# Heads of two edge loops: a store and a memset out of the barrier, index loads on SyncE, chunk loads ahead of stores, first rows ahead of chunk 3

## What is computed

```
x = layernorm(x + L0(x));  x = layernorm(x + L1(x))

L0: w   = silu(silu(emb(length) @ w0 + b0) @ w1 + b1) @ w2 + b2      # per edge
    msg = products of w, x_up[src] and the unit vector of the edge     # per edge, 2 x 128
    out = segment_sum(msg, dst) @ W_out / 16
L1: h   = relu(concat(x[src], x[dst]) @ W1[type] + b1[type]) @ W2[type] + b2[type]
    msg = h * sigmoid(concat(x[src], x[dst]) @ attn_w[type] + attn_b[type])
    agg = segment_sum(msg, dst);  GRU(agg, x) + x, then layernorm, gamma, beta
```

## Time and profile before

| | us |
|---|---|
| median of 3 runs | 2268.96 (2262.18 to 2270.72) |
| profiled execution, time | 2275.48 |
| profiled execution, span | 2273.8 |
| busy: TensorE / VectorE / ScalarE / GpSimd | 1808.1 / 1479.4 / 1340.5 / 1602.6 |

### The profile page before, as it was taken

One profiled execution on the slowest core, in us unless ns is written; L12 is line 12 of the kernel. 1 busy time (PEld: TensorE's weight loads), 2 busy tenths in 40 slices (PEclk: granted clock), 3 DMA queues, 4 the chain that ended last, 5 costly groups with the idle time before them and its releaser, 6 DMA issues.

```text
span 2273.8 us, 43703 instructions
## 1 busy us (share of the span) xinstructions
PE 1808.1 (80%) x10012; PEld 1435.9 (63%) x10012; DVE 1479.4 (65%) x3700; ACT 1340.5 (59%) x4414; POOL 1602.6 (70%) x1699
## 2 busy tenths in 40 slices
PE   7497999999999999999857776676766667666674
PEld 4275666676666666666636666666666656666563
DVE  4656556556555556556535677777777777778775
ACT  2486778778777777778624544454544445544442
POOL 2567777777777777777544777777777777777771
PEclk6599999999999999999968998788888888888886
DMA  6522223223233232323256854445455454454451
GB/s 204 146 52 56 73 79 82 77 74 87 74 83 79 74 84 75 81 79 82 70 163 167 218 144 115 115 113 121 108 117 119 108 122 113 114 118 113 116 115 34
DMA packets 222343, 236.65 MB, mean 104 GB/s; under 512 B 73015, under 2 KB 163295, under 8 KB 222157
## 3 DMA queue, kind: packets, MB, share of 16 engines
q0 software_dynamic: 53808, 112.80, 21.5%
q10 hardware_dynamic: 90588, 58.98, 10.2%
q1 hardware_dynamic: 77905, 64.42, 9.5%
HBM read 191.66 MB, written 44.35 MB: 104 GB/s over the span
## 4 chain that ended last, share of the span: by engine, by line
POOL 24%; issue 14%; DMA 5%; PE 3%; DVE 2%; ACTq 1%; ACT 1%; POOLq 0%; SPq 0%; DVEq 0%
POOL gp L601 24%; DMA gp<-p_tab_d,idx 2%; DMA win<-q_tab_d 1%; PE ps_v L1760 1%; PE ps_e L1721 1%; ACTq L1517 1%; DVE hid L1867 1%; DMA q_tab_d<-unit_area 0%; ACT hid L1625 0%; DMA unit_area<-x_t_d 0%; ACT unit_area L1655 0%; DMA q_tab_d<-acc 0%; DVE acc L1955 0%; DMA key_row<-key_row_d 0%; DMA zero<-x_t_d 0%
## 5 line engine op out<-in xcount | busy, mean ns | idle before, releaser
L601 POOL DMA_INDIRECT gx<-node_d,idx x832 | 793.9, 954 | 278.9 <-issue 255.7
L601 POOL DMA_INDIRECT gp<-p_tab_d,idx x832 | 791.2, 951 | 277.2 <-issue 248.9
L673 ACT ACTIVATE msg<-ws,y 128x32 f32<-128x32 f32 x2496 | 550.0, 308 | 75.5 <-DVE ws L652 75.1
L894 PEld LDWEIGHTS ps_a<-hot,msg 128*128 128x128 f32 x3328 | 409.3, 198 | 203.2 <-issue 107.3
L1721 PE MATMUL ps_e<-win,hot_x 128*128 128x129 f32 x1680 | 299.8, 351 | 280.3 <-DVE hid L1867 261.3
L894 PE MATMUL ps_a<-hot,msg 128*128 128x128 f32 x3328 | 432.6, 285 | 70.4 <-DVE msg L661 49.0
L1721 PEld LDWEIGHTS ps_e<-win,hot_x 128*128 128x128 f32 x1680 | 274.8, 256 | 303.0 <-DVE hid L1867 274.9
L655 DVE TENSOR_TENSOR vy<-gx,y 128x768 f32<-128x768 f32 x104 | 99.7, 959 | 354.7 <-DMA gx<-node_d,idx 354.5
L1625 ACT ACTIVATE hid<-hid,score 128x128 f32<-128x128 f32 x832 | 277.6, 393 | 10.1
L1867 DVE TENSOR_TENSOR hid<-ps_e,gp 128x387 f32<-128x387 f32 (+1 forms) x312 | 142.0, 508 | 151.8 <-DMA gp<-p_tab_d,idx 142.5
L634 PE MATMUL ps_w<-w,h 128*128 128x256 f32 x832 | 219.6, 409 | 0.0
(11 more groups left out here) (220 smaller groups left out, 2209.1 us busy)
## 6 DMA issues: line engine op xcount, KB each, us to landing
win<-q_tab_d ACTq DMA_DIRECT2D x416, 64.5 KB
key_row<-key_row_d ACTq DMA_DIRECT2D x102, 256.0 KB, 3.7
gx<-node_d,idx POOLq DMA_INDIRECT x832
gp<-p_tab_d,idx POOLq DMA_INDIRECT x832
p_tab_d<-acc SPq DMA_DIRECT2D x23, 516.0 KB, 3.3
q_tab_d<-unit_area SPq DMA_DIRECT2D x36, 258.0 KB, 4.2
q_tab_d<-acc SPq DMA_DIRECT2D x5, 774.0 KB, 4.5
emb<-emb_d SPq DMA_DIRECT2D x102, 32.0 KB
```

Source lines behind the costliest of these rows:

```text
L601: e.indirect_dma_start(out=buf[:, h, t, :], out_offset=None, in_=table, in_offset=bass.IndirectOffsetOnAxis(ap=idx[:, h, t:t + 1], axis=0) ...
L673: last = e.activation(self.cols[1][:, tile, c, :], self.ws[:, tile, :], ACT.Copy, scale=y[:, c:c + 1])
L894: last = e.matmul(ps_a[:, h, b, :], msgs[h].tile(t, b), hot[:, h, t, :], start=t == 0, stop=t == TPS - 1)
```

## The change

- In `prepare`, the zero tile is stored ahead of the sixteen embedding stores, behind the memset of `zero` (semaphore `clear`). SyncE no longer waits there for the embedding stores: it does so in `edges0`, ahead of the first embedding loads, and ScalarE ahead of each `clear_high`.
- VectorE's wait for `row_st` and its memset of 4228 columns leave `prepare`. ScalarE clears 2052 + 1664 of these columns behind its key-row store; the 512 columns from which that store reads are cleared by VectorE in `edges0`, behind the messages of step 0 and the wait for `row_st`.
- In `edges0`, SyncE loads the indices of steps 4 and 5 first, then waits for the embedding stores, loads two embedding tiles, then the index of step 6, then the weights. In the loop the index load comes ahead of the embedding load; the first four steps stand ahead of the loop, with only the index of step 7 in them.
- In `edges1`, SyncE loads the indices of steps 4 to 7: 4 and 5 behind the windows of step 1, 6 ahead of the store of chunk 4, 7 behind it. ScalarE's first four steps load none.
- The node loads of later chunks go ahead of the chunk's store (`store_first`) or of its third piece (`store_table`); the key rows of steps 2 and 3 go ahead of the windows of step 0.
- ScalarE makes the rows of step 0 behind chunk 2, ahead of chunk 3, and waits for `b_ok` only before the node updates. VectorE clears the place of chunks 0 to 2 behind step 0 and that of chunks 3 and 4 inside step 1.

The diff, cut of declarations:

```diff
@@ -60,6 +60,7 @@
 LAG = 3
 LOOPS = STEPS // SLOTS
 N_LATER = 25
+KEY_AT = 2 * TPS * P + PPS
...
@@ -175,6 +176,7 @@
         h1=m.sb("h1", [P, HALF]), h2=m.sb("h2", [P, HALF]),
         ps_h=m.ps("ps_h", [P, HALF]), ps_x=m.ps("ps_x", [P, 512]), ps_w=m.ps("ps_w", [P, 2, TPS, H]),
         h1_mm=m.sem("h1_mm"), h1_ok=m.sem("h1_ok"), h2_mm=m.sem("h2_mm"), h2_ok=m.sem("h2_ok"), w_mm=m.sem("w_mm"),
+        emb_st=m.sem("emb_st"), row_st=m.sem("row_st"),
...
@@ -361,6 +364,8 @@
                 e.dma_start(start_r.bitcast(i32), a["start"].rearrange("o (j q) -> (o j) q", q=PPS))\
                     .then_inc(ld_row, 16)
 
+                e.wait_ge(clear, 1 + 3 + 1)
+                e.dma_start(dram["emb"][STEPS], k["zero"][0:2 * NB, :]).then_inc(stored, 16)
                 for n, span in enumerate(spans):
                     e.wait_ge(exp_ok, n + 1)
                     first, steps = span.start // HALF, (span.stop - span.start) // HALF
@@ -369,9 +374,7 @@
                         e.dma_start(dram["emb"][at_step:at_step + steps].rearrange("s r n -> r s n"),
                                     emb[2 * NB * g:2 * NB * (g + 1), span].rearrange("r (s n) -> r s n", s=steps))\
                             .then_inc(emb_st, 16)
-                e.dma_start(dram["emb"][STEPS], k["zero"][0:2 * NB, :]).then_inc(stored, 16)
                 e.wait_ge(stored, 16 * 3)
-                e.wait_ge(emb_st, 16 * ECH)
                 e.wait_ge(ld_w, 16 * 10)
...
@@ -421,6 +424,9 @@
                 layer0_silu(e, w, mlp, 2, 2)
                 e.wait_ge(row_ok, 1)
                 e.dma_start(dram["key_row"], key_r).then_inc(row_st, 16)
+                e.wait_ge(clear, 1 + 3 + 1)
+                for span in (slice(0, KEY_AT), slice(keys, scratch)):
+                    e.activation(acc[:, span], k["zero"][:, 0:1].to_broadcast([P, span.stop - span.start]), ACT.Copy)
...
@@ -445,7 +451,7 @@
                 e.memset(w["w1"][:], 0.0).then_inc(clear, 1)
                 e.memset(w["w2"][:], 0.0).then_inc(clear, 1)
                 e.memset(w["b2_1"][:], 0.0)
-                e.memset(k["zero"][:], 0.0)
+                e.memset(k["zero"][:], 0.0).then_inc(clear, 1)
...
@@ -539,8 +545,6 @@
                 e.sem_inc(hits_ok, 1)
                 own.then(e.scalar_tensor_tensor(k["key"][:], k["key"][:], 1.0, hit[:], ALU.add, ALU.mult))
                 own.did(e.tensor_scalar(k["key"][:], k["key"][:], 1.0, None, ALU.subtract))
-                e.wait_ge(row_st, 16)
-                e.memset(acc[:, 0:scratch], 0.0)
                 e.wait_ge(count_ok, 1)
                 e.tensor_scalar(k["n_left"][:], ps_n[:], -1.0, float(P * TILES), ALU.mult, ALU.add)
...
@@ -744,13 +748,13 @@
                     e.sem_inc(gate_x, 1)
                     e.dma_start(dram["x1_t"][:, bass.ds(g * UN, UN)], v["x1_t"]).then_inc(xt_st, 16)
 
-                def steps(i, unit, before, last=False):
+                def steps(i, unit, before, last=False, idx_from=0):
                     for u in range(SLOTS):
+                        if not last and u >= idx_from:
+                            e.wait_ge(landed[u], i * (16 * TPS) + 16 * TPS)
+                            load_idx(i * SLOTS + (u + SLOTS), u)
                         if not last:
                             load_emb(i * SLOTS + u, 1 - u % 2)
-                        if not last:
-                            e.wait_ge(landed[u], i * (16 * TPS) + 16 * TPS)
-                            load_idx(i * SLOTS + (u + SLOTS), u)
...
+                def early_idx(u):
+                    e.wait_ge(landed[u], 16 * TPS)
+                    load_idx(SLOTS + u, u)
+
+                for u in range(SLOTS - 2):
+                    early_idx(u)
+                e.wait_ge(mlp["emb_st"], 16 * ECH)
                 for h in range(2):
                     e.dma_start(emb[:, 1 - h, :], dram["emb"][h + 3]).then_inc(emb_in[1 - h], 16)
+                early_idx(SLOTS - 2)
...
@@ -770,7 +782,8 @@
                 load_x(0)
                 for u in range(SLOTS):
                     e.dma_start(k["idx1"][:, u, :], dram["p_idx"][:, u * TPS:(u + 1) * TPS]).then_inc(k["idx_in1"][u], 16)
-                with e.Fori(0, LAG) as i:
+                steps(0, False, False, idx_from=SLOTS - 1)
+                with e.Fori(1, LAG) as i:
                     steps(i, False, False)
...
@@ -812,6 +825,7 @@
                 assert CLEAR * LAG * SLOTS == T * NACC - v["end"]
 
                 def clear_high(j):
+                    e.wait_ge(mlp["emb_st"], 16 * ECH)
                     e.activation(k["acc"][:, bass.ds(j * CLEAR + v["end"], CLEAR)],
                                  k["zero"][:, 0:1].to_broadcast([P, CLEAR]), ACT.Copy)
...
-                e.sem_inc(acc_own, 2)
+                e.sem_inc(acc_own, 1)
...
@@ -1098,8 +1112,11 @@
                 e.tensor_copy(ps_a[:, :, IOTA, :], spread(k["iota"][:, 0:P], 1, 2)).then_inc(iota_ok, 1)
                 e.wait_ge(iota_ok, 1)
                 one_hot(0, 0)
-                for u in range(SLOTS):
-                    messages(0, u, first=u == 0)
+                messages(0, 0, first=True)
+                e.wait_ge(mlp["row_st"], 16)
+                e.memset(k["acc"][:, KEY_AT:KEY_AT + TPS * P // 2], 0.0).then_inc(acc_own, 1)
+                for u in range(1, SLOTS):
+                    messages(0, u)
...
@@ -1535,18 +1553,19 @@
                         load_xq(c + 2)
 
                 def store_first(c):
+                    next_xq(c)
                     e.wait_ge(q_ev, 2 * CH * (c + 1) + 2)
                     if c >= CH:
                         e.wait_ge(q_first[c % CH], 16 * (c // CH))
                     e.dma_start(q_g[:, c * CH:(c + 1) * CH, :], first_buf[:, c * CH:(c + 1) * CH, :])\
                         .then_inc(q_first[c % CH], 16)
-                    next_xq(c)
 
                 def store_table(c):
                     for s in range(CH):
+                        if s == CH - 1:
+                            next_xq(c)
...
 
                 for s in q_st:
                     e.sem_inc(s, 16)
@@ -1554,15 +1573,26 @@
                     load_xq(c)
                 for h in range(2):
                     load_row(e, h, h)
-                for c in range(2):
-                    store_first(c)
-                    e.wait_ge(q_first[c], 16)
-                    load_windows(e, regs, c, c)
+                def early_idx(u):
+                    e.wait_ge(landed[u], 16 * TPS)
+                    load_idx(e, SLOTS + u, u)
+
+                store_first(0)
                 for h in range(2):
                     e.wait_ge(hx_ok, h + 1)
                     load_row(e, h + 2, h)
+                e.wait_ge(q_first[0], 16)
+                load_windows(e, regs, 0, 0)
+                store_first(1)
+                e.wait_ge(q_first[1], 16)
+                load_windows(e, regs, 1, 1)
+                for u in range(2):
+                    early_idx(u)
                 for c in range(2, AHEAD):
+                    if c == AHEAD - 1:
+                        early_idx(2)
                     store_first(c)
+                early_idx(3)
                 for c in range(AHEAD, CHUNKS):
                     store_table(c)
...
@@ -1662,12 +1692,13 @@
                         for s in range(CH):
                             e.wait_ge(q_st[s], 16 * (c - AHEAD + 2))
 
-                def steps(i, unit, before, last=False, table=False):
+                def steps(i, unit, before, first=False, last=False, table=False):
                     for u in range(SLOTS):
                         j, h = i * SLOTS + u, u % 2
                         if table:
                             table_out(j + (AHEAD - 1), CH - 1)
-                        rows(j, h)
+                        if not first or u > 0:
+                            rows(j, h)
                         if table:
                             table_out(j + AHEAD, 0)
...
-                        if not last:
+                        if not last and not first:
                             e.wait_ge(landed[u], i * (16 * TPS) + 16 * TPS)
                             load_idx(e, j + SLOTS, u)
...
                 e.preload_act_table(ACT.Sigmoid)
-                e.wait_ge(b_ok, 1)
                 for c in range(AHEAD):
+                    if c == CH:
+                        rows(0, 0)
                     for s in range(CH if c < AHEAD - 1 else CH - 1):
                         table_out(c, s)
                 for i in range(LAG):
-                    steps(i, False, False, table=True)
+                    steps(i, False, False, first=i == 0, table=True)
                 table_out(CHUNKS - 1, CH - 1)
                 chunk_stored(CHUNKS - 1)
+                e.wait_ge(b_ok, 1)
                 steps(LAG, True, False)
...
-                def edge_rows(i, u, before):
+                def clear_first(lo, hi):
+                    for c in range(lo, hi):
+                        e.wait_ge(q_first[c % CH], 16 * (c // CH + 1))
```

(14 more changed lines are left out.)

11 lines of the change are left out of this document (6 added, 5 removed).

## The result

The changed kernel took **2253.68 us** (median of six runs, 2245.87 to 2257.98), the kernel before 2268.73 us beside it (six runs, 2262.18 to 2270.72): ratio 0.9934, 95% interval 0.9911 to 0.9957. That is 15.05 us faster where 35.1 had been forecast, and above the range, which ended at 2249. The profiled execution has a span of 2253.1 us, 20.7 less than the one before. All of them are less than the forecast.

A forecast was written before the change was run, and what follows sets the result against it. GpSimd's gathers were taken as the bound, so holes removed between them count one for one: 9.8 + 9.3 in layer 0 and 16 in layer 1 make 35.1 us, from 2268.96 to 2234 us, range 2224 to 2249.

The forecast's parts named there:

- Hole 1: Barrier before layer 0: without the key-row store wait and VectorE's clear, the loop's first gather comes 9.8 us earlier.
- Rival (b): Barrier before layer 0: SyncE or ScalarE arrives late, hole 1 gives 3 us instead of 9.8, so 2241; chance 0.05.
- Hole 2: Head of layer 0's loop: the wait for step 4's index, the first reloaded one, goes whole, 9.3 us.
- marks that would tell against the forecast: Heads of both layers: gathers over 1.25 us on average, step 8's index wait over 10 us, or holes at steps 9 to 12.
- Moved clears: Both heads: the clears that now fall among gathers cost the gathers nothing.
- Hole 3: Head of layer 1: index 8 goes out 11.5 to 14.7 us earlier, step 8 waits 3 to 7; 16 us gained.
- (a): Layer 1's head: the stall is handed on, index 8 moves only 0 to 8 us; about 2246 us; chance 0.11.
- (c): Moved clears: VectorE's clears lock the gathers out, 7 us late, so 2241 us; chance 0.02.
- (d): Layer 0's loop: SyncE's wait for gathers delays embedding loads, slower kernel, 2294 us at 0.6 us a step; chance 0.03.
- (e): Both heads: held by something the profile doesn't name, change within 0.5% (11.3 us); chance 0.03.

The follow-up runs named there:

- only_layer1: The kernel before with layer 1's part of the change alone: 2257.93 us, ratio 0.9950.
- without_layer1: The changed kernel with layer 1 as in the kernel before (preparation and layer 0 changed): 2256.64 us, ratio 0.9959.
- index8_11_2: The changed kernel with SyncE also loading layer 1's indices of steps 8 to 11: 2242.37 us, ratio 0.9854; on the first chip (before there: 2999 us) 2982.36 us, 0.9943.
- the second and third comparisons: The unaltered changed kernel timed again against the kernel before: 2244.91 us, ratio 0.9897, then 2248.48 us, ratio 0.9893.

## Why the prediction was wrong

The direction, all places and the bound (the gathers) were right. Of the forecast's 35.1 us, the profiles show some 20 to 21. Step by step:

**Hole 1, 9.8 us: wrong, 4.5 in the first pair, 2.2 in later profiles.** "GpSimd comes last, and the same 1.01 us later its next gather starts" counted from the end of the last gather's record. GpSimd does come last, but the 1.01 us belong to the end of its drain, which ends 3 to 6 us after that record. Before, it lay under VectorE's clear, 3.8 us short of it: a cover that was taken away without asking what stood under it. It was to be read from the trace of before (68.8 + 25.6). This is the failed step: the drain was put at nothing and takes 5.3 us in the first pair of profiles. There the loop's first gather came 6.6 us later than forecast, 5.3 by the drain and 1.3 by a later end of the gathers. Rival (b), at 0.05, had the size of it (3 us), but with late SyncE or ScalarE as the cause, and these were ready at 85.4. A second error lies in the base: 10.77 us was one execution's hole, others have 3.8 to 6.4, and the median of before, from which the sum was made, need not contain it. On the profiles of the usual speed with clock 0.64 to 0.70 the step is worth 6.4 - 4.2 = 2.2 us.

**Hole 2, 9.3 us: right for the wait, but 4 us of it given back.** The wait is gone (9.99 to 10.85 us from step 3 to 4). Yet steps 3 to 24 as a whole take 215.6 us in place of 220.6 and 220.9 (only_layer1): 5.1 us gained. The rest went into gathers held up by VectorE's product. While gathers run without a pause and VectorE catches up behind them, at 8.13 us a step, the product's start is not tied to a gather, and it meets one each step: 1.83 us for the slow one and its pause, five more at 1.25, 8.1 in all, so that the meeting repeats itself. In the steady state VectorE waits for a gather, which ties the product's start to the gathers, at a harmless place: in after the wait of 3.90 us ends with the product's start at 563.47, 0.20 us behind a gather's start at 563.27, and that gather takes 0.94 us. Taking the index wait away left GpSimd with more work to do ahead of VectorE, and the stretch of meetings grew: gathers of steps 3 to 23 are 1.3 and 2.2 us too long in sum with the old order, 4.9 to 5.8 in the changed kernel and without_layer1 (7.1 in index8_11_2). That more work ahead of VectorE is what lengthens the stretch is argued from these rows; no run varied it alone. "If gathers in a head take more than 1.25 us each on the average" stood among the marks that would tell against the forecast, and it came: steps 3 to 11 of after take 94.75 us for 72 gathers, 1.32 us each.

**Moved clears: right.** No gather is longer for a memset or for one of ScalarE's clears: the one of 1.77 us beside ScalarE's first clear (82.98) starts inside VectorE's L546, and before has the same one without that clear (82.88, 1.77 us). The lockout of GpSimd by VectorE that was weighed there does act in this kernel, in operations that the change doesn't touch.

**Hole 3, 16 us: right in mechanism and in the first pair (15.7), 13.2 on the average.** Index 8 was issued 93.35 us after step 0's first gather (1250.38, 1157.03) and is now issued 80.16 us after it (1229.47, 1149.31): 13.2 us earlier, inside the 11.5 to 14.7. Step 8 waits 6.08 us, inside the 3 to 7; in five other profiles of the new layer 1 on the usual chips it waits 4.6 to 7.2. Only the base was high again: with the old layer 1, steps 0 to 8 took 101.55, 98.02 and 96.49 us, mean 98.7; with the new, 84.2 to 86.8 in six profiles, mean 85.5. So 13.2 us on the average.

**The sum.** 2.2 + 5.1 + 13.2 = 20.5 us, against ratios of 0.9934, 0.9897 and 0.9893 (15.0, 23.4 and 25.1 us). The first comparison, 15.05 us, has an interval of 10 to 20 us, so that 20.5 lies at its upper end; what made it lower than the later two stays open, the share of executions with the slower preparation being one candidate. So corrected, the forecast would be 2248.5 us, near the upper end of the range: of the miss of 19.8 us, 14.6 are the steps' (7.6 the barrier, 4.2 hole 2, 2.8 layer 1), and the other 5 aren't explained.

**Rivals.** (a), the stall handed on in layer 1, didn't come in this change, and came in index8_11 on the first chip. (c) had the right mechanism at the wrong operation. (d) shows no trace: steps are 10.0 us as before. (e), a gain within 0.5%, is left out by the second and third comparisons (upper ends 0.9922 and 0.9914). The range was too narrow for a sum whose terms had been read from one execution that was itself 6.5 us over the median: that distance had to lie somewhere, and likely part of it lay in the holes that the forecast gave back in full (10.77 us where other profiles have 3.8 to 6.4, and 101.55 against 98.0 and 96.5 in layer 1).

## What to carry to other kernels

Where a wait is removed from a barrier, list when each engine's own end comes (its drain, not its last operation; behind gathers, their last packet): the gain ends at the second latest. Where the profiled execution lies above the median, its holes are suspects; take a second profile before a hole of a few us is counted in full. And where an engine that gathers is freed of a wait, look at which VectorE operations with SBUF operands alone it will now meet.

## What the runs showed of the hardware

- At the end of a block GpSimd's drain ends 2.8 to 3.8 us after its last gather's record in the profiles with a granted clock of 0.64 to 0.70 from 25 to 50 us (5.7 in one of them), and 4.9 to 6.5 us in those with 0.50. With the last gather 13 us earlier it ended 13 us earlier. In all 17 profiles it ends 1.3 to 2.0 us after the last packet of these gathers.
- A gather that starts inside a VectorE operation with two SBUF operands, or with one at the rate of 0.55 us for 768 columns, is longer by the rest of that operation less 0.12 to 0.14 us. At the product vy this holds from 0.036 us after its start on; one that starts within 0.032 us of it isn't held. Behind one with an operand in PSUM, a memset or a reciprocal a gather stays at 0.94 to 0.96 us.
- Executions prepare in two ways, and the changed kernel's own profiles show both: TensorE granted 0.50 or 0.64 to 0.70 of its clock from 25 to 50 us, the first gather at 53 to 56 or at 49.7 to 52.8 us.
